# Scores over three PSUM banks, block projections in one, value products in one step: an attention and expert kernel on one core

## What is computed

```python
q = einsum('bse,hde->bhsd', xn, Wq) + bq;  k, v likewise
scores = where(causal, -inf, einsum('bhsd,bhtd->bhst', q, k) / 8)
att = softmax(scores) / 8
attention = einsum('bhst,bhtd->bhsd', att, v).reshape(b, s, 1024) @ proj
logits = l2norm(xn @ Wp.T + bp) @ l2norm(sim) * exp(min(temp, ..))
lw = softmax(logits);  ret = lw where it is the largest, else 0
out = x + attention + xn @ W.T + sum_e ret_e * (xn @ Wd_e.T @ Wu_e.T)
```

## Time and profile before

| | us |
|---|---|
| median of 3 runs | 1488.75 |
| lowest and highest | 1488.54, 1489.19 |
| the profiled execution | 1484.91 |
| its span, first to last instruction | 1482.8 |
| TensorE busy | 1433.1 (97%) |
| GpSimd busy | 1351.0 (91%) |
| VectorE busy | 1161.3 (78%) |
| ScalarE busy | 1057.0 (71%) |

### The profile page before, as it was taken

How to read it: one execution, slowest core, us unless ns; L and a number is a source line. 1 busy time by engine, 2 the same in 40 slices (tenths; PEclk the granted TensorE clock), 3 DMA queues, 4 the chain that set the end, 5 groups by cost and what they waited for, 6 DMA issues and landing times. The chain is left out here.

```text
span 1482.8 us, 40863 instructions
## 1 busy us (share of the span) xinstructions
PE 1433.1 (97%) x11036; PEld 1146.4 (77%) x11036; DVE 1161.3 (78%) x4134; ACT 1057.0 (71%) x3032; POOL 1351.0 (91%) x1414
## 2 busy tenths in 40 slices
PE   6999999999999999999999999999999999999998
PEld 5678777777877778778787787878778787777876
DVE  6787878878788787887878778787887878878784
ACT  4777777767777676776777777777777777777774
POOL 5999989999899998999989999998999999999996
PEclk9999999999999999999999999999999999999999
DMA  6444443443444344344443544444444344434431
GB/s 156 106 94 105 101 110 88 103 113 92 105 104 107 90 99 118 88 109 97 107 100 91 123 92 99 104 104 104 91 102 112 92 110 103 107 85 106 108 86 51
DMA packets 112932, 150.65 MB, mean 102 GB/s; under 512 B 18175, under 2 KB 47166, under 8 KB 112830
## 3 DMA queue, kind: packets, MB, share of 16 engines
q1 hardware_dynamic: 112830, 149.68, 42.8%
HBM read 11.20 MB, written 4.19 MB: 10 GB/s over the span
## 5 line engine op out<-in xcount | busy, mean ns | idle before, releaser
L535 POOL TENSOR_SCALAR prob<-prob,rden 128x128 f32<-128x128 f32 (+3 forms) x1024 | 1092.2, 1084 | 81.6 <-DVE rden L798 59.4
L809 DVE CUSTOM_DVE_ANT_0 prob<-scores,mask 128x128 f32<-128x128 f32 (+3 forms) x1024 | 461.6, 485 | 261.3 <-issue 220.1
L613 ACT ACTIVATE prob<-prob,nmax 128x128 f32<-128x128 f32 (+3 forms) x1024 | 564.4, 554 | 102.5 <-DVE nmax L809 99.5
L1060 PE MATMUL ptp<-ident,prob 128*128 128x128 f32 x2560 | 379.3, 275 | 13.7 <-DVE pt L821 9.6
L624 ACT ACTIVATE pt<-ptp 128x128 f32<-128x128 f32 (+3 forms) x512 | 222.1, 434 | 189.7 <-PE ptp L1060 176.5
L1048 PE MATMUL scores<-k_twice,q_parts 128*128 128x128 f32 (+3 forms) x1024 | 332.8, 335 | 17.5 <-DVE nmax L809 9.0
L1084 PE MATMUL zp<-pt,v_sb 128*64 128x64 f32 (+3 forms) x4096 | 335.8, 306 | 0.8 <-DVE z_lo L827 0.8
L1060 PEld LDWEIGHTS ptp<-ident,prob 128*128 128x128 f32 x2560 | 294.8, 140 | 52.0 <-issue 17.6
L1051 PE MATMUL scores<-k_low,q_parts 128*128 128x128 f32 (+3 forms) x1024 | 321.9, 324 | 0.0
L1048 PEld LDWEIGHTS scores<-k_twice,q_parts 128*128 128x128 f32 x1024 | 193.5, 189 | 84.5 <-issue 30.6
L1084 PEld LDWEIGHTS zp<-pt,v_sb 128*64 128x64 f32 x4096 | 210.2, 137 | 53.4 <-issue 43.7
(11 more groups left out here) (141 smaller groups left out, 1703.4 us busy)
## 6 DMA issues: line engine op xcount, KB each, us to landing
k_twice<-k_hi SPq DMA_DIRECT2D x512, 128.0 KB, 2.4
q_parts<-q_hi SPq DMA_DIRECT2D x256, 128.0 KB, 2.4
q_parts<-q_lo SPq DMA_DIRECT2D x256, 128.0 KB, 2.4
xin<-in_L_attn_x_dram SPq DMA_DIRECT2D x16, 256.0 KB, 3.1
xres<-in_L_attn_x_dram SPq DMA_DIRECT2D x16, 256.0 KB, 2.9
out_dram<-osb SPq DMA_DIRECT2D x16, 256.0 KB, 2.5
pt<-in_L_attn_Wq_dram SPq DMA_DIRECT2D x1, 512.0 KB, 4.3
pt<-in_L_attn_Wk_dram SPq DMA_DIRECT2D x1, 512.0 KB, 4.6
```

The costliest lines, as they stand in the source:

```text
L535: nc.gpsimd.tensor_scalar(part, part, rden[:, s % NROT, h:h + 1], None, ALU.mult)\
L613: nc.scalar.activation(part, part, ACT.Exp, bias=nmax[:, s % NROT, h:h + 1], scale=-1.0, accum_out=den[:, s % NROT, h:h + 1]).then_inc(p_r ...
L809: nc.vector.tensor_tensor_reduce(out=prob[:, s % NROT, h, 0:cols], in0=scores[h][:, 0:cols], in1=mask[:, S - cols:S], scale=-INV_SCALE, sc ...
L1060: done = nc.tensor.transpose(ptp[h][:, P * j:P * j + P], prob[:, s % NROT, h, P * j:P * j + P], ident[:])
```

## The change

- `bank_of(s)` is 0: all jobs share one bank, `jobp[0]`. The bank that is won goes to the scores: `scores` has three, and head `h` of step `s` takes bank `(2 * s + h) % 3`. It waits for the maximum of the head that used that bank last, three heads back.
- `LAG_PV = (9, 9)`: the value products of both heads stand in the second step of a pair, 32 matmuls in a row.
- TensorE issues the job of a step straight after the transposes, ahead of value products and output quarters. The output quarters all stand in fourth steps.
- VectorE takes out a `q` at the start of its step, ahead of the maxima; all other jobs are taken out where they were.
- `router` moves from step 5 to 1 and `gated` from 26 to 21, both now in second steps like `xt` (25). Two `v` blocks move, from 29 to 26 and from 21 to 22. The base product, the experts' product and the router's chain on VectorE move with them (`STEP_BASE`, `STEP_LORA`, `R_FIRST`).
- The finished sum is transposed back through `zp`.
- GpSimd normalises with `tensor_tensor` and a broadcast reciprocal where it had `tensor_scalar`; two waits for things long done go away.

```diff
-LAG_PV = (8, 9)
+LAG_PV = (9, 9)
-LAG_OUT = ((27, 31, 35, 39), (25, 27, 31, 35))
+LAG_OUT = (23, 27, 31, 35)
-JOBS[5] = ("router", 0)
+JOBS[1] = ("router", 0)
-JOBS[26] = ("gated", 0)
-V_STEPS = (29, 30, 2, 6, 10, 14, 18, 21)
+JOBS[21] = ("gated", 0)
+V_STEPS = (26, 30, 2, 6, 10, 14, 18, 22)
-STEP_EVAC, STEP_BASE, STEP_OUT, STEP_FINAL, STEP_LORA = 20, 23, 22, 23, 29
+STEP_EVAC, STEP_BASE, STEP_OUT, STEP_FINAL, STEP_LORA = 20, 22, 23, 24, 24
-R_FIRST = 23
+R_FIRST = 15
+NSCORE = 3
+LAST_HEAD = 2 * UNITS - 1
+def score_bank(n):
+    return 1 if n == LAST_HEAD else n % NSCORE
 def bank_of(s):
-    return s % 2
+    return 0
...
                 for h in range(2):
                     part = prob[:, s % NROT, h, 0:width(s)]
-                    nc.gpsimd.tensor_scalar(part, part, rden[:, s % NROT, h:h + 1], None, ALU.mult)\
-                        .then_inc(pn_ready, 1)
+                    scale = rden[:, s % NROT, h:h + 1].to_broadcast([P, width(s)])
+                    nc.gpsimd.tensor_tensor(part, part, scale, ALU.mult).then_inc(pn_ready, 1)
...
             def step(c, s, first=False, last=False, tail=False):
+                made = JOBS.get((s - 1) % UNITS, (None,))[0]
...
                 if not tail:
+                    if made == "q":
+                        evacuate_job()
                     maximum(c, s)
...
-                if s > 0 and s - 1 in JOBS and not (last and s - 1 in AHEAD):
-                    job(c, s - 1)
-                if s == 0 and not first:
-                    job(c, UNITS - 1, back=1)
+                if made not in (None, "q"):
+                    evacuate_job()
...
+                    n = 2 * s + h
+                    dst = scores[score_bank(n)]
-                    wait(pe, sm_ready, c.head(s - 1, h))
+                    wait(pe, sm_ready, c.at(2 * UNITS, score_before(n) + 1))
...
                     transpose(c, unit)
+                if not tail and s in JOBS and not (last and s in AHEAD):
+                    job(c, s)
...
-                if s in JOBS and not (last and s in AHEAD):
-                    job(c, s)
```

More of the change, by code:

```diff
@@ L202, in sem @@
             return ctx.enter_context(nc.semaphore(name))
-        scores = [psum(f"scores{h}") for h in range(2)]
+        scores = [psum(f"scores{n}") for n in range(NSCORE)]
         ptp = [psum(f"ptp{h}") for h in range(2)]
@@ L208, in build @@
         outp = psum("outp")
-        jobp = [psum(f"jobp{n}") for n in range(2)]
-        weight_banks = [*scores, *ptp, zp, outp]
+        jobp = [psum("jobp")]
+        weight_banks = [*scores[0:2], *ptp, zp, outp]
         w_hi = [sb(f"w_hi{n}", [P, H * DH], F32R) for n in range(3)]
@@ L911, in step, with evacuate_job @@
             def step(c, s, first=False, last=False, tail=False):
+                made = JOBS.get((s - 1) % UNITS, (None,))[0]
+                def evacuate_job():
+                    if s > 0 and not (last and s - 1 in AHEAD):
+                        job(c, s - 1)
+                    if s == 0 and not first:
+                        job(c, UNITS - 1, back=1)
                 if not tail:
+                    if made == "q":
+                        evacuate_job()
                     maximum(c, s)
@@ L1018, in _ @@
                     pe.wait_ge(w_lo_ready, 4)
-                    pe.wait_ge(bqk_ready, 1)
                 if kind == "v":
@@ L1068, in values @@
                     wait(pe, z_ready, c.pair(p - 1))
+                if h == 0 and LAG_PV[0] + NBLK * p == STEP_OUT + 2:
+                    wait(pe, final_ready, c.at(1, 0))
                 if h == 0 and p in (0, NPAIR // 2):
-                    for bank in range(2):
+                    for bank in range(len(jobp)):
                         made = [js for js in V_STEPS[:4] if js not in AHEAD] if p == 0 else V_STEPS[4:]
@@ L1112, in transpose_sum @@
             def transpose_sum(c, tail):
-                bank = bank_of(STEP_OUT)
-                if not tail:
-                    pe.wait_ge(job_done[bank], c.job(STEP_OUT))
+                pe.wait_ge(z_ready, c.pair(-1 if tail else (STEP_OUT - LAG_Z) // NBLK))
                 pe.wait_ge(y_copied, c.at(1, 0))
@@ L1120, in transpose_sum @@
                     cols = slice(P * i, P * i + P)
-                    done = nc.tensor.transpose(jobp[bank][:, cols], y_t[:, cols], ident[:])
+                    done = nc.tensor.transpose(zp[:, cols], y_t[:, cols], ident[:])
                 done.then_inc(y_ready, 1)
@@ L1135, in step @@
                     for quarter in range(4):
-                        n = due(s, OCT_STEPS * o + LAG_OUT[o][quarter], UNITS, first, tail)
+                        n = due(s, OCT_STEPS * o + LAG_OUT[quarter], UNITS, first, tail)
                         if n is not None:
```

33 lines of the change are left out of this document (17 added, 16 removed).

## The result

| | us |
|---|---|
| median of 4 runs, changed kernel | 1916.64 |
| lowest and highest | 1908.50, 1926.54 |
| the kernel before beside it, median of 4 | 1488.64 |
| ratio, with its 95% interval | 1.288 (1.281 to 1.295) |
| the profiled execution and its span | 1926.54, 1924.7 |

The change makes the kernel 29% slower. The time lies within the range, 1.1% above the forecast.

A forecast was written before the change was run, and what follows sets the result against it. TensorE's pace was taken to bound the kernel at 90.25 us a batch. 90.25 - 2.7 - 3.1 + 17.0 + 12.3 + 2.1 = 115.8, times 16 plus 41 gives 1894, put at 1895; range 1790 to 2000.

The forecast's parts named there:

- The wait at `q`: In every pair TensorE stands at `q` until VectorE ends `v_sb` and frees the one bank: 1.93 us.
- `k` after `q`: `k` waits for VectorE to take `q` out of the one bank: 0.2 us a pair.
- The second-step jobs: `router`, `xt`, `gated` await `k`, 1.55 us each; `v` then awaits them, 2.24, 3.04, 2.36: 12.3 us a batch.
- The plain pair: A pair without a second-step job was expected to take 12.2 us in the changed kernel's timeline.
- The router's chain: Its VectorE pieces in third and fourth steps lie in TensorE's path: 2.1 us a batch, range 0.9 to 3.
- The clock stays: The forecast itself: both kinds of wait come and TensorE's granted clock does not fall; 1895 us, chance 0.74.
- the clock falls in the longer waits: Rival: TensorE's clock drops after waits near 3 us; 1945 once a batch, 2045 in all three pairs; chance 0.13.
- GpSimd's instruction: Normalising with two inputs takes 1040 ns over 128x512 against 1563; the saving meets no wait, worth 0.
- old waits: TensorE's idle time on scores' banks, GpSimd and `k_twice`, 3.1 us a batch, taken off in full.
- Value products: Both heads' value products in a row save TensorE some 0.34 us a pair, 2.7 a batch.
- Only the fourth step waits: Rival: VectorE is ahead in second steps, so the 12.3 and half the chain go; 1683 us, chance 0.07.
- The waits do not bite: Rival: `v_sb` is out before TensorE reaches `q`, only gains remain; 84.4 us a batch, 1395; chance 0.03.

The follow-up runs named there:

- e13: The kernel before with both heads' value products in the second step of a pair and GpSimd normalising by tensor_tensor: 1423.95 us, ratio 0.958.
- e6: The kernel before with one edit, GpSimd normalising by tensor_tensor with a broadcast reciprocal: 1442.75 us, ratio 0.972.
- e4: The changed kernel, one job bank, with VectorE taking out v as well as q ahead of the maxima: 1784.94 us, ratio 1.204.
- e2: The changed kernel, one job bank, with VectorE taking out every job at the start of its step, ahead of the maxima: 1661.94 us, ratio 1.120.

## Why the prediction was right or wrong, point by point

**The wait at `q`: right.** 2.24 + 0.10 - 0.4 = 1.93 us a pair was the term; measured are 2.28, 0.06 and 0.4, which makes 1.94. The list of waits reads 222.1 / 128 = 1.74, less by 0.2 because it counts from the end of the transposes and not from the time at which the next instruction could have started.

**`k` after `q`: right.** 0.2 was the term, 0.19 is measured.

**The second-step jobs: nearly right.** From the start of the six transposes to that of the job pass 2.20 us for `xt` and `gated` and 2.13 for `router`; less their 0.65 the waits for `k` are 1.55, 1.55 and 1.48 (term 1.55 each). From the eight transposes to `v` pass 2.81 behind `router`, 3.01 behind `gated` and 3.61 behind `xt`; less 0.79 that is 2.02, 2.22 and 2.82 (terms 2.24, 2.36, 3.04). Together 11.6, against 12.3. The largest misses are `v` behind `router` and behind `xt`, 0.22 each.

**The plain pair: right.** 12.3 (12.2 in the list of what to look for) was expected and 12.26 to 12.35 is what it takes. It can also be had from below: e13's plain pair 10.03 + 1.93 + 0.19 = 12.15.

**The router's chain: too large.** The sum was 115.8 a batch; with the waits filled it is 113.45. Of the difference of 2.35, 0.65 is in the jobs above, and if the other terms hold, the other 1.7 leaves some 0.4 of the 2.1 set for the chain. The lower bound of 0.9 was for the one dear piece in a fourth step, 939 ns in the earlier trace rows; but that was the stretched instruction shown above, beside a GpSimd at work. In the changed kernel GpSimd is idle at that place, and the same instruction takes

```profile
L917 DVE CAST gated_parts<-gated 128x256 fp32r<-128x256 f32 x16 | 4.5, 283 | 0.0
```

It stands between the maxima and `v_sb`, so its 0.28 is on the path that TensorE waits for, and the pair that holds it measures 0.33 longer (12.60 to 12.27). The place was read rightly, and the duration was taken from a row in which another engine had its part.

**The clock stays: wrong.** It had 0.74 of the chance, and the time came out near it by luck, because this error and those of the sum nearly cancel: 16 x (115.8 - 113.45) = 38 us too much, 62 too little, and 1895 - 38 + 62 = 1919 against 1916.64. The rival "the clock falls in the longer waits" had the mechanism, at 0.13, with a single fall for 1945. Its step "the wait at `xt` is just as long" looked for a wait of 3 us, the one in the earlier trace rows; the falls come with waits of 1.8 to 2.6, and with the longest, the one at `v` behind `xt`, only in 4 of 15 batches. "Here it has a full load on both sides of the wait", the reason that spoke against it, was worth nothing: TensorE is busy up to each of these waits. Its price was too high: half of a 3.4 us stretch is 1.7 us, but the pair of `gated` takes 18.69 with a stretch at its `q` and 17.44 without, so 1.25, and 54 of these make an estimated 68 us against the 69.5 between the profiled executions. Where a part of the rest goes can be seen: in the slow stretch at 569.65 above, `k` starts 0.40 after its transposes and not 0.63, so its wait of 0.2 is gone.

The Trainium skill (TensorE: Matmul & The Clock Gate, HAM oscillation) warned of a fall in every round. By the traces that is what happens, in every batch at least twice, and the filled waits show that it can be cured without taking a wait away; the upper end of 2045 that I gave for the rule was too high by some 130 us.

**GpSimd's instruction: time right, worth wrong.** 1042 ns at 512 columns where the earlier trace rows let expect 1040. But "a saving there meets no wait" looked at GpSimd's share of the batch, 84 us in more than 110, and not at who stands behind it at one place of the batch. It is worth about 10 us by itself and 28 with the clock. In the sum it was hidden in the "old waits", which were taken off in full.

The Trainium skill (GPSIMD Engine Reference, Engine selection) would have the new instruction be the slower one; three kernels now say the opposite, by 42, 28 and 10 us.

**Old waits: the size from the wrong column.** 3.1 us a batch is TensorE's idle time, and that of the whole span: a good part of the 49.7 us lies in setup and tail, which the 41 us had already. Over fourteen batches (98.18 to 1365.24) TensorE is idle for 1267.06 - 1241.64 = 25.4 us, 1.8 a batch. On the other side e6 wins 2.65 a batch by GpSimd alone, half of it out of busy time, so there was more to be had than idle time shows. In the kernel before, both edits together win (1486.9 - 1423.95) / 16 = 3.9 a batch, where the sum took off 3.1 + 2.7 = 5.8; the rest of the 5.8 was absorbed by the new waits, since 113.45 less the new waits of 17.0 and 11.6 is 84.8 a batch, less than e13's 86.5. That last step is worked out, and no run shows it by itself.

**Value products: right in size, with a condition.** 2.34 us for 32 of them, and 0.28 to 0.37 in four of the eight pairs, where 0.34 was computed; the other four give back a part. "That gain is real in either case" was too much: with the old instruction on GpSimd it is a loss of 21 us.

**The other rivals.** "Only the fourth step waits" fell: `k_lo` is behind every second-step job. "The waits do not bite" named VectorE taking jobs out ahead of the maxima as what would bring it about; e4 and e2 tried just that, and the chain through one bank still costs 12%.

**Open.** Why the clock falls with some waits and not with others is not settled, and length alone does not decide it: none of the 73 waits of 1.7 us at `q` brought a fall and all 14 of 2.0 did, but `v` behind `router` waits 1.8 us and brought none in 15 batches, and `v` behind `xt` waits 2.6 and brought 4. Nor is what lengthens the first pair in e13.

## What to carry to other kernels

A buffer is paid for by the longest way from its being filled to its being emptied, not by how often it is used: before two users are put on one bank, read from the timeline when the consumer ends, and subtract what the producer has to do until then. Before two edits that look independent are judged, look whether the engine that one of them relieves is what makes the other one pay; value products together cost 21 us alone and won 19 beside a faster GpSimd. And of waits of 2 us that come back in every round, price the clock too: filler matmuls tell in one run what it costs.

## What the runs showed of the hardware

- On GpSimd, multiplying fp32 rows by one value each takes 1563 ns over 128x512 with the value as a scalar operand and 1042 with it broadcast as a second input; over 128x128 the new one takes 401. The rows of the changed kernel, by shape:

```profile
L551 POOL TENSOR_TENSOR prob<-prob,rden 128x512 f32<-128x512 f32 x256 | 261.3, 1042 | 307.8 <-DVE rden L812 307.8
...
L551 POOL TENSOR_TENSOR prob<-prob,rden 128x128 f32<-128x128 f32 x256 | 97.2, 401 | 15.1 <-DVE rden L812 14.2
```

- TensorE's granted clock fell to 0.50 with waits of 1.8 to 2.6 us in the midst of dense work, 50 times in 1925 us, and filling the waits with matmuls that do nothing brought 0.942 up to 0.993 and the time down by 62 us.
- 97% busy does not mean that TensorE never waits: the same 11036 matmuls read 1433.1 us busy with a slow GpSimd and 1410.8 with a fast one.
- The same VectorE instruction (a cast over 128x256, 0.28 us) took 1.03 us in 14 batches of the kernel before, ending 0.15 us after the GpSimd instruction that ran beside it. A duration that is carried over to another kernel wants a look at what the other engines did at that moment.
